# Decoder layer with dense experts on one core: a list of first steps for each engine, and three pairs' exponentials taken straight from PSUM

## What is computed

```
x = layernorm(x + attention(x))            # 16 sequences x 128 tokens x 256, 16 heads of 16
x = layernorm(x + xattn(x, ctx))           # a recurrence over the 128 tokens: exp(k), exp(-k), exp(u+k)
x = layernorm(x + experts(x))              # 8 experts of 256 -> 1024 -> 256
# softmax(scores) @ v;  the experts' gate: every token goes to each of the 8 experts (K = 128 = S),
# out = sum_e gate[e] * (gelu(x @ W1[e] + b1[e]) @ W2[e] + b2[e])
```

## Time and profile before

| | before |
|---|---|
| median of 3 runs | 941.93 us (941.58 to 944.29) |
| the profiled execution | 941.72 us, of which the span is 940.0 us |
| PE busy | 899.2 us (96%) |
| DVE busy | 598.8 us (64%) |
| ACT busy | 573.8 us (61%) |
| POOL busy | 78.8 us (8%) |

### The profile page before, as it was taken

One profiled execution on the slowest core, in us unless ns is written; L12 is line 12 of the kernel. 1 busy time (PEld: TensorE's weight loads), 2 busy tenths in 40 slices (PEclk: granted clock), 3 DMA queues, 4 the chain that ended last, 5 costly groups with the idle time before them and its releaser, 6 DMA issues.

```text
span 940.0 us, 17996 instructions
## 1 busy us (share of the span) xinstructions
PE 899.2 (96%) x6738; PEld 819.9 (87%) x6738; DVE 598.8 (64%) x1254; ACT 573.8 (61%) x983; POOL 78.8 (8%) x116
## 2 busy tenths in 40 slices
PE   6789888999999999999999999999999999999997
PEld 5678888889988988999988999889998999899997
DVE  6788888877656575655676464755766564433574
ACT  6437875786555565666556765655556665444684
POOL 4220011000110010100120001200110000000000
PEclk8899999999999999999999999999999999999999
DMA  7248998867655554555545564555546455665340
GB/s 237 90 159 271 358 388 287 298 217 250 226 172 165 161 179 146 160 167 158 179 136 170 158 188 146 164 163 166 170 124 190 149 167 172 193 185 167 113 136 12
DMA packets 144694, 172.45 MB, mean 183 GB/s; under 512 B 11208, under 2 KB 110816, under 8 KB 144608
## 3 DMA queue, kind: packets, MB, share of 16 engines
q1 hardware_dynamic: 144176, 171.16, 57.1%
q10 hardware_dynamic: 432, 0.14, 0.1%
HBM read 135.60 MB, written 35.65 MB: 182 GB/s over the span
## 4 chain that ended last, share of the span: by engine, by line
PE 86%; DVE 7%; ACT 4%; issue 1%; DMA 1%; POOL 0%; SPq 0%; POOLq 0%; DVEq 0%; ACTq 0%
PE down_ps L757 13%; PE down_ps L758 12%; PE down_ps L759 12%; PE up_ps L522 12%; PE up_ps L524 12%; PE up_ps L523 12%; PE bank L584 2%; PE bank L522 1%; PE bank L566 1%; PE bank L544 1%; PE bank L524 1%; PE bank L523 1%; ACT h_all L895 1%; PE bank L602 1%; DVE neg_max L1030 1%
## 5 line engine op out<-in xcount | busy, mean ns | idle before, releaser
L895 ACT ACTIVATE h_all<-up_ps,b_all 128x512 f32<-128x512 f32 (+1 forms) x296 | 183.3, 635 | 261.1 <-PE up_ps L524 259.6
L957 DVE TENSOR_TENSOR h_lo<-h_all,h_hi 128x512 fp32r<-128x512 f32 x256 | 177.9, 695 | 223.0 <-ACT h_hi L886 222.3
L757 PE MATMUL down_ps<-w_hi,h_hi 128*128 128x256 f32 x1024 | 295.7, 289 | 2.9 <-DVE acc L1149 2.9
L758 PE MATMUL down_ps<-w_lo,h_hi 128*128 128x256 f32 x1024 | 290.3, 283 | 0.0
L759 PE MATMUL down_ps<-w_hi,h_lo 128*128 128x256 f32 x1024 | 290.1, 283 | 0.0
L522 PE MATMUL up_ps<-x2t_hi,w_hi 128*128 128x512 f32 (+1 forms) x592 | 221.7, 374 | 3.2 <-ACT h_all L895 3.1
L524 PE MATMUL up_ps<-x2t_hi,w_lo 128*128 128x512 f32 (+1 forms) x592 | 216.4, 365 | 0.0
L523 PE MATMUL up_ps<-x2t_lo,w_hi 128*128 128x512 f32 (+1 forms) x592 | 215.7, 364 | 0.0
L757 PEld LDWEIGHTS down_ps<-w_hi,h_hi 128*128 128x128 f32 x1024 | 195.8, 191 | 11.5 <-issue 2.0
L758 PEld LDWEIGHTS down_ps<-w_lo,h_hi 128*128 128x128 f32 x1024 | 196.5, 192 | 6.8
L759 PEld LDWEIGHTS down_ps<-w_hi,h_lo 128*128 128x128 f32 x1024 | 196.3, 192 | 0.0
(11 more groups left out here) (199 smaller groups left out, 999.6 us busy)
## 6 DMA issues: line engine op xcount, KB each, us to landing
w_hi<-w_parts SPq DMA_DIRECT2D x200, 256.0 KB, 3.1
w_lo<-w_parts SPq DMA_DIRECT2D x200, 256.0 KB, 3.3
w_raw<-in_w_dram SPq DMA_DIRECT2D x96, 256.0 KB, 4.0
w_parts<-w_hi SPq DMA_DIRECT2D x64, 256.0 KB, 3.9
w_parts<-w_lo SPq DMA_DIRECT2D x64, 256.0 KB, 4.2
x_in<-in_x_dram SPq DMA_DIRECT2D x8, 256.0 KB, 4.2
ctx_sb<-in_ctx_dram SPq DMA_DIRECT2D x8, 256.0 KB, 3.8
out_dram<-acc SPq DMA_DIRECT2D x8, 256.0 KB, 2.6
```

The lines of the kernel that those rows point to most:

```text
L757: nc.tensor.matmul(ps, hi, w2h[:, c, :], start=c == 0 and j == 0, stop=False, skip_group_check=True)
L758: nc.tensor.matmul(ps, hi, w2l[:, c, :], start=False, stop=False, skip_group_check=True)
L895: a = nc.scalar.activation(h_all[:, unit % HALL, k * wide:(k + 1) * wide], up_ps[unit % 2][:, k * wide:(k + 1) * wide], ACT.Gelu_apprx_tan ...
L957: return nc.vector.tensor_tensor(dst, src, hi.bitcast(F32), ALU.subtract)
```

## The change

All in tables and waits; the mathematics stays. (1) TensorE, ScalarE, VectorE and GpSimd each get a list of their own. DIAG_1 goes ahead of M_0; the gate's constants (`wg_both`, `b2_all`) are made after ATT instead of ahead of M_2, and `decay_row` after M_3; GpSimd splits the values before it adds the bias to x, and splits all seven weight pieces in one go. (2) Pair 0's attention uses seven PSUM banks for turned probabilities and values. (3) The first `DIRECT` = 3 pairs, so pairs 1 and 2 as well, take exponentials from PSUM: VectorE's shift goes, ScalarE runs eight exponentials a unit where it ran two, and TensorE's T_0 and T_2 wait until the exponentials of both units are through, since they write over the scores. (4) E_0 and E_1 of pair 1 go behind items 0 and 1; in `EARLY` E_0, E_1, E_2 and E_3 are parted by an item, pair 2's X goes from item 26 to 24, QK from 29 to 28, Q_LOW ahead of DIAG_0. (5) A copy (`spare`) in each layernorm goes; three small loads go from ScalarE's queue to SP's; the fillers ahead of item 0 are arranged anew.

```diff
@@ exponentials (ScalarE)
-                    if s == EXPS[u] and first(p):
+                    if s == EXPS[u] and direct(p):
...
-                            act.wait_ge(max_ready, g + (3 if u == 2 else 1))
+                            act.wait_ge(max_ready, QUADS * p + g + (1 if u % 2 or first(p) and u == 0 else 3))
...
-                    if s == EXPS[u] and not first(p):
+                    if s == EXPS[u] and not direct(p):
@@ maxima and shift (VectorE)
-                        for i in range(0 if first(p) else 2):
+                        for i in range(0 if direct(p) else 2):
@@ turned probabilities (TensorE)
-                    pe.wait_ge(shifted, QUADS * (p - 1) + 2 * u + 4)
+                    if direct(p):
+                        pe.wait_ge(probs_ready, QUADS * p + 2 * u + 4)
+                    else:
+                        pe.wait_ge(shifted, QUADS * (p - DIRECT) + 2 * u + 4)
@@ layernorm (VectorE)
-                nc.vector.tensor_copy(spare[:, which:which + 1], stats[:, 0, 1:2])
@@ fillers (TensorE)
                 if (p, s) == (0, BACK):
-                    idle_products(bank[1], 7)
-                if (p, s) == (1, S_1):
-                    idle_products(bank[1], 2)
-                if (p, s) == (0, R_TURN):
-                    idle_products(up_ps[1], 4)
+                    idle_products(bank[1], 14)
@@ tables
-FIRST_ROUTE = {0: [1], 6: [4], 8: [5]}
-FIRST_SPLIT = {(0, V): [(0, 0), (0, 1), (0, 2)], (0, E_1): [(0, 3), (1, 0)], (0, ATT): [(1, 1), (1, 2)]}
+FIRST_ROUTE = {0: [1], 1: [2, 3], 6: [4], 8: [5]}
+FIRST_SPLIT = {(0, V): [(0, 0), (0, 1), (0, 2)], (0, E_1): [(0, 3), (1, 0), (1, 1), (1, 2)]}
-SETUP_AT, DECAY_AT = DIAG_1, T_0
+SETUP_AT, DECAY_AT = ATT, M_3
+DIRECT = 3
```

More of the change, by code:

```diff
@@ L506, in _ @@
                     for p, s in steps(FIRST_ITEM[n] + k):
+                        if s == X_BIAS and second(p):
+                            load_x(p + 1)
                         if s == QK and p > 1 and p + 1 < NPAIR:
@@ L590, in weigh_values @@
                     pe.wait_ge(v_step, 5 * (p + 1))
-                if first(p) and u < 2:
+                if first(p) and u >= 2:
                     pe.wait_ge(probs_ready, QUADS)
-                if first(p) and u >= 2:
-                    pe.wait_ge(att_ready, u - 1)
                 for i in range(2):
@@ L775, in _ @@
             pe.wait_ge(masks_made, MASKS)
[L776 removed]
+            for p, s in FIRST_PE:
                 attend(p, s)
@@ L1327 @@
 EARLY = [
-    {T_0: 1, T_1: 1, W_0: 4, W_1: 5, S_2: 8, M_2: 8, S_3: 8, M_3: 8, E_2: 11, E_3: 11, T_2: 14, T_3: 15, W_2: 17, W_3: 18, ATT: 20, CTX: 20,
+    {E_0: 0, E_1: 1, T_0: 2, T_1: 3, W_0: 5, W_1: 6, X_BIAS: 6, S_2: 8, M_2: 8, S_3: 8, M_3: 8, E_2: 10, E_3: 11, T_2: 14, T_3: 15, W_2: 17, W_3: 18, ATT: 20, CTX: 20,
      WO: 22, NORM1: 24, Y1: 26, XEXP: 26, REC_0: 26, REC_1: 27, REC_2: 28, REC_3: 28, BACK: 31, NORM2: 31, R_TURN: 33,
      R_LOGITS: 35, R_MAX: 36, R_GATE: 41, R_GATE_T: 50, R_BIAS: 51},
-    {X: 26, X_LOW: 27, X_BIAS: 27, QK: 29, K_COPY: 29, Q_COPY: 29, K_LOW: 30, DIAG_0: 32, Q_LOW: 32, V: 32, V_ADD: 34, V_SPLIT: 35,
-     S_0: 37, M_0: 37, S_1: 37, M_1: 37, DIAG_1: 40, E_0: 41, E_1: 41, T_0: 44, T_1: 45, W_0: 48, W_1: 49, S_2: 53, M_2: 53, S_3: 53, M_3: 53, E_2: 57, E_3: 57,
+    {X: 24, X_LOW: 25, X_BIAS: 27, QK: 28, K_COPY: 28, Q_COPY: 28, K_LOW: 30, Q_LOW: 31, DIAG_0: 33, V: 32, V_ADD: 34, V_SPLIT: 35,
+     S_0: 37, M_0: 37, S_1: 37, M_1: 37, DIAG_1: 40, E_0: 41, E_1: 42, T_0: 44, T_1: 45, W_0: 48, W_1: 49, S_2: 53, M_2: 53, S_3: 53, M_3: 53, E_2: 57, E_3: 58,
      T_2: 60, T_3: 61, W_2: 64, W_3: 65, ATT: 68, CTX: 69, WO: 71, NORM1: 73, Y1: 76, XEXP: 76, REC_0: 76, REC_1: 77, REC_2: 79,
@@ L1346 @@
           15: [(1, 0, 3)]}]]
[L1348 to L1359 removed]
+FIRST_PE = ([(0, s) for s in (X, QK, V, S_0, S_1, S_2, S_3, T_0, T_1, W_0, T_2, W_1, T_3, W_2)]
+            + [(1, X), (0, W_3), (0, ATT), (0, CTX), (0, WO), (1, QK), (0, Y1), (1, V), (0, BACK), (0, R_TURN), (1, S_0), (1, S_1)])
+FIRST_ACT = ([(0, s) for s in (K_COPY, V, E_0, E_1, E_2, T_0, T_1, E_3, T_2, T_3)]
+             + [(1, X), (0, ATT), (0, CTX), (1, K_COPY), (0, XEXP), (1, Q_COPY), (0, R_TURN)])
+FIRST_DVE = ([(0, s) for s in (K_LOW, DIAG_0, Q_LOW, K_LOW_1, Q_LOW_1, DIAG_1, M_0, V_ADD, M_1, M_2, M_3, T_0, T_1, W_0, W_1, T_2, T_3, W_2)]
+             + [(0, W_3), (1, X_LOW), (0, ATT), (0, WO), (0, NORM1), (1, K_LOW), (0, REC_0), (0, REC_1), (0, REC_2), (0, REC_3), (1, V_ADD),
+                (0, BACK), (1, DIAG_0), (0, NORM2), (1, Q_LOW), (0, R_TURN), (1, DIAG_1), (1, M_0), (1, M_1)])
+FIRST_POOL = [(0, V_SPLIT), (0, X_BIAS), (0, WO), (0, BACK), (1, V_SPLIT)]
+FIRST_ROUTE = {0: [1], 1: [2, 3], 6: [4], 8: [5]}
+FIRST_SPLIT = {(0, V): [(0, 0), (0, 1), (0, 2)], (0, E_1): [(0, 3), (1, 0), (1, 1), (1, 2)]}
+FIRST_SPLIT_LOW = {(0, X_BIAS): [(0, 0), (0, 1), (0, 2), (0, 3), (1, 0), (1, 1), (1, 2)]}
+SETUP_AT, DECAY_AT = ATT, M_3
+DIRECT = 3
 PROJECTIONS = (1, 0, 2, 3)
```

50 lines of the change are left out of this document (24 added, 26 removed).

## The result

| | before | changed |
|---|---|---|
| median, measured side by side, 10 runs each | 942.81 us (941.26 to 945.99) | 947.06 us (944.44 to 947.83) |
| ratio, 95% interval | | 1.0034 (1.0018 to 1.0050) |
| the profiled execution, its span | 941.72, 940.0 us | 946.98, 945.3 us |
| PE, DVE, ACT busy | 899.2, 598.8, 573.8 us | 900.6, 587.5, 588.4 us |

The changed kernel is slower by 3.2 us by the ratio (1.7 to 4.7 us); the medians lie 4.3 us apart, the two profiled executions 5.3. The forecast was +3.0 us, with 0.40 on slower. VectorE lost 11.3 us of work and ScalarE got 14.6 more, as forecast (some 10 and some 15).

The account below looks back on a forecast made before the run. Bound: the first up product's start, then TensorE's waits and clock losses up to 200 us. Terms: -3.25 (to R_TURN of pair 1) + 2.95 (pair 2's waits) + 3.3 (half clock) = +3.0 on 941.72, 944.7 us; range 937.0 to 948.5.

Parts of the forecast that it names:

- 0.40 on slower: Whole kernel: chance given to a measurably slower result, against 0.33 for the same and 0.27 for faster.
- The early gain: Before the experts: 5.5 us won at the first up product, of which 2.2 are left by item 7.
- The first up product: End of the stretch before the experts: starts at about 57.0 us instead of 62.53, 5.5 us earlier.
- I take nothing: Before the experts: VectorE beside GpSimd's w_lo run could lose 0 to 4 us; the sum counted none.
- the rival with 0.15: Before the experts: GpSimd's long run slows VectorE; with 3.5 us lost the end is at 948; chance 0.15.
- Items 0 to 20: Pair 1's parted exponentials and loads give most back: T_0 at 69.7, T_2 at 97.0, 1.65 us late at item 12.
- Items 20 to 36: VectorE binds and is relieved by 4.9 us, so R_TURN of pair 1 comes at 140.9 us, 3.25 earlier.
- Pair 2: Items 36 to 62: PSUM exponentials make T_0 and T_2 wait 3.3 and 2.7 us; 2.95 net, plus 3.3 for clock.
- 2.95 + 3.3: Pair 2, items 36 to 62: 2.95 us of net waiting plus 3.3 us for two stretches at half clock.
- if its clock stays up after 3 us of waiting: Sign of being wrong: TensorE's clock was forecast to fall behind pair 2's waits, costing 1.65 us each.
- the third rival: Pair 2: the clock holds at its waits, so 3.3 us go and the time is 941.4, no change; chance 0.13.
- The gain-kept rival: Items 0 to 20: T_0 of pair 1 before 66 us, loads hidden, 5.5 us kept, end at 937.5; chance 0.27.

Follow-up runs that it names:

- e3: Changed kernel with pair 1's E_0, E_1 and gate exponential grouped ahead of the first item, E_2 and E_3 at item 11, still from PSUM: ratio to before 0.9985.
- e1: Changed kernel with DIRECT = 1: pairs 1 and 2 take exponentials from shifted scores in SBUF, only pair 0 from PSUM: ratio to before 0.9908.
- e6: Changed kernel with DIRECT = 2: pair 2 takes exponentials from shifted scores in SBUF, pairs 0 and 1 from PSUM: ratio to before 0.9952.
- e12: Changed kernel with the three small loads back on ScalarE's queue and the decay rows behind the attention step: ratio to before 1.0020.
- e2: Changed kernel with VectorE's four decay rows made behind the attention step (ATT) instead of after M_3: ratio to before 1.0004.
- e8: Changed kernel with exponentials from PSUM for pair 0 alone and decay rows behind the attention step (e1 and e2 together): ratio to before 0.9887.
- e9: Changed kernel with PSUM exponentials for pair 0 alone, late decay rows and pair 1's exponentials grouped (e8 plus e3): ratio to before 0.9846, 928.9 us.
- e4: Kernel before with DIRECT = 3 and its waits alone (pairs 0 to 2 from PSUM), old lists and item tables: ratio to before 1.0088.
- e7: Changed kernel with 26 idle 128x512 products on TensorE in front of T_0 of pair 1: ratio to before 1.0018.
- e11: Changed kernel with the three small loads issued from ScalarE's queue again instead of SP's: ratio to before 1.0030.

## Why the forecast came out as it did

**Right in mechanism; the closeness of the sum is partly luck.** The sum was worked out on the profiled execution of the kernel before. On the profiled executions the change costs 5.3 us, 2.3 more than forecast, and these 2.3 arise before item 12 (below). That the ratio says 3.2 is within what it can tell (1.7 to 4.7), but its 0.2 us from the forecast are luck. The early gain is given back where the forecast said. T_0 of pair 1 waits 7.45 us (forecast 8) for E_1, with two loads between the units; pair 2's waits are 3.23 and 2.61 us (forecast 3.3 and 2.7). e3 shows that the parted order with its loads is a cause (4.6 us), e1 and e6 that reading from PSUM is, by longer units and a later T_0 together (4.1 us for pair 1, 7.7 for pair 2).

**The first up product: 58.3, not 57.0.** Two terms were wrong, with opposite signs. The forecast let E_1 end "as before at 19.8 us". But E_1 had waited 0.57 us for its maxima, and with S_1 earlier (14.63 against 16.24 us) it stands right behind E_0 and ends at 19.05; S_2 starts at 17.20 instead of 20.34, and E_3 ends at 27.0 instead of the 28.2 that I worked out. The moved small loads, which had no part in the sum, move S_1, but little of that comes through E_0 (e12). And for GpSimd beside VectorE, "I take nothing": the four `decay_row` lasted 4.77 us, and e2 prices this at 2.2 us of the first product (1.5 by e8 against e1). That was the rival with 0.15; its mechanism was there, at the place named (`decay_row` outlasts the wait for `pt_hi`), at about the 2 us named as decisive. The earlier end of E_1 hid part of it. The Trainium skill, "GPSIMD Engine Reference", section "1. Specifications", names VectorE operations with two SBUF inputs or in a two-port mode as those that share; `decay_row` reads one tensor and one value per partition and was slowed to 1.19 us each. Which of the two cases it is, no run here shows.

**Items 0 to 20: carried over one for one.** The chain from the first gelu took 11.1 us (10.9). The later first product and 0.7 us more between T_0 and T_2 put T_2 at 99.20 instead of 97.0 and the gelu of item 12 at 101.49 instead of 99.25: 3.9 us late, not 1.65. This is the whole miss of the forecast in the profiled execution (946.98 against 944.7). The step that was mis-sized is thus the first up product, by "I take nothing".

**Items 20 to 36: right, and not because VectorE shifts less.** From the gelu of item 12 to R_TURN the changed kernel wins 4.6 us (forecast 4.9). e9 has the shifts and wins as much from T_2 to R_TURN (44.5 us against before's 49.2, 44.2 in the changed kernel); e4, with old tables and no shifts, wins 0.4. VectorE's gap of 2.15 us is still there in e4 (2.30 us before 140.91) and gone in the changed kernel and in e9. So the tables pay, as the terms of the sum had it; no run moves pair 2's X, QK and Q_LOW alone. Only where the units are parted do the shifts cost there: 46.8 us in e1, 44.2 in e6.

**Pair 2: the sum right, its parts not.** From R_TURN to the end the profiled execution loses 6.1 us; the forecast said 2.95 + 3.3 = 6.25. But I took from the two waits of 3.3 and 2.7 us the 1.22 and 1.30 us of waiting on `acc` that would go. In e6, without pair 2's waits, these go as well (0.43 us is left at the first): the tables remove them, not the PSUM exponentials. So the price of pair 2 is 7.7 us, and the tables give some 2 back. The subtractions themselves were off too: 3.3 - 1.22 is 2.08 and 2.7 - 1.30 is 1.40, where the sum used 1.8 and 1.15 without a row for the difference.

**The clock: sometimes.** The same waits stand in seven profiled executions (changed, e2, e3, e4, e7, e11, e12; 3.2 and 2.6 us, in e4 2.2 and 2.1). Behind T_0 of pair 2 the clock fell in four of them, behind T_2 in four. In e2 it did not, with TensorE as busy and as long idle:

```profile
165.50:169.00 3.50, 3.46 (x30) 1.00 0.51 184
195.70:199.00 3.30, 3.29 (x29) 1.00 0.03 7
```

Ahead of T_0, from R_TURN on, TensorE had been busy for 19.80 of 23.40 us in the changed kernel and for 19.78 of 23.43 in e2. What decides between the two outcomes no run showed. The forecast's sign of being wrong, "if its clock stays up after 3 us of waiting", thus came true in two of the six executions that waited 3.2 us at T_0 (e2 and e7), though not in the changed kernel's own. So the third rival was half true.

What a fall costs can be read where the same stretch ran both ways. From T_0 to T_2 of pair 2, the changed kernel and below it e2; then from T_2 to R_TURN of pair 1, the changed kernel and below it e3:

```profile
166.79:198.50 31.71, 29.10 (x220) 25.56 (x220) 19.10 (x35) 23.05 (x48) 0.00 (x0) 0.94 0.70 230
165.54:195.72 30.18, 27.55 (x221) 24.00 (x221) 19.03 (x35) 22.96 (x48) 0.00 (x0) 1.00 0.69 230
99.20:143.39 44.19, 39.91 (x344) 39.25 (x345) 38.88 (x78) 36.59 (x73) 4.22 (x6) 0.96 0.99 337
93.93:138.14 44.21, 38.65 (x344) 37.73 (x345) 38.87 (x78) 36.54 (x73) 4.23 (x6) 1.00 1.04 359
```

At T_0 of pair 2 the fall costs 1.5 us, and at T_2 1.5 again (R_TURN of pair 2 comes 45.7 us behind it in the changed kernel, 44.2 in e2): 3.0 for both, where the forecast had 3.3. With eight falls in fourteen, the mean is a little over half of that. From T_2 to R_TURN of pair 1 the fall costs nothing, although TensorE works 1.3 us longer: there it waits for VectorE in the end (2.64 us for `q_lo`).

**The gain-kept rival** fell as described: nothing passes the loads and E_1. But e1 shows what it would have needed: a T_0 that waits for the first unit alone, and shorter units.

## What to carry to other kernels

Split a change that moves the time little into its parts before judging it: here lists worth 5 to 9 us carried exponentials that cost 8 to 12, and the best version (928.9 us) keeps the lists, with the decay rows later, the old exponentials for all pairs but the first, and their grouping. Saving one engine work by giving another more pays only if the second isn't waited for there: VectorE's 11 us were nearly all slack, while much of ScalarE's 15 stood in front of TensorE. And an operation that is moved into a gap must be costed beside what runs on its neighbour there, not by its row elsewhere.

## What the runs showed of the hardware

- Four 128x128 `decay_row` operations on VectorE, SBUF to SBUF, took 4.77 us beside GpSimd's run of `w_lo` and 0.86 us alone. That is 1.19 us each, about the length of one `w_lo` (8.62 / 7 = 1.23); the pair of `pt_lo` that read PSUM took 1.29 us beside the same run and 1.28 us later without it.
- A wait of TensorE can cost more than its length. With the same waits of 3.2 and 2.6 us at pair 2, the stretch from T_0 to T_2 took 31.7 us where the clock fell behind T_0 (changed, e11, e12) and 30.2 where it held (e2, e7). Where VectorE was waited for next, a fall cost nothing: 44.2 us from T_2 to R_TURN of pair 1 at a clock of 0.96 (changed) and of 1.00 (e3).
- After a wait of 7.45 us the clock was at its lower level in each of the five profiled executions that had it, and after the same interval filled with 26 idle products it stayed at the upper one. After the wait of 4.5 us at T_2 of pair 1 it fell in six of six. After 2.1 to 3.3 us at T_0 and T_2 of pair 2 it fell in eight of fourteen cases, and after the 2.3 to 2.6 us at R_TURN of pair 1 in ten of the fourteen executions.
- Over all runs of a kernel the mean granted clock was 0.9802 in the changed kernel, 0.9866 in e1 and 0.9900 in e9. The 0.0098 between the outer two would be 9 us of 940, half of the 18 us between their medians, if all of it lay where TensorE was needed; at R_TURN of pair 1 some of it did not.
